# The split of the expert weights, moved: eight pieces of W1 early, W2 beside the groups, twelve pieces behind the last group

## The reference

```python
W = jnp.zeros((d, d)).at[rows, cols].set(w_est)
x = x + layernorm(x) @ W
z = layernorm(x);  xn = layernorm(z) * gamma + beta
w = softmax(top_2(xn @ Wr + br))                # 2 of 8 experts a row
for e in range(8):
    h = gelu(xn @ W1[e] + b1[e])                # 256 -> 512
    y = y + (h @ W2[e] + b2[e]) * w_full[e]     # 512 -> 256
x = x + y
```

## Time and profile before

| what | us |
|---|---|
| median of 3 runs | 1062.63 (1062.45 to 1066.76) |
| the profiled execution | 1061.05 |
| its span, first to last instruction | 1059.3 |
| PE busy | 900.6 |
| DVE busy | 753.9 |
| ACT busy | 633.8 |
| POOL busy | 627.9 |

### The profile page before, as it was taken

How to read it: one execution, slowest core, us unless ns; L and a number is a source line. 1 busy time by engine, 2 the same in 40 slices (tenths; PEclk the granted TensorE clock), 3 DMA queues, 4 the chain that set the end, 5 groups by cost and what they waited for, 6 DMA issues and landing times. The chain is left out here.

```text
span 1059.3 us, 25594 instructions
## 1 busy us (share of the span) xinstructions
PE 900.6 (85%) x6756; PEld 840.9 (79%) x6757; DVE 753.9 (71%) x2315; ACT 633.8 (60%) x1325; POOL 627.9 (59%) x490
## 2 busy tenths in 40 slices
PE   2583889898886029999999999999999999999992
PEld 1123777787775029999999999999999999999992
DVE  6985798999973507777777777777777777777761
ACT  2254666667662006776776776676676676677661
POOL 3664077777777743475565665665666564656653
PEclk9696899889986559999999999999999999999996
DMA  5055376766734533455544644544544554544542
GB/s 159 22 158 168 87 220 200 232 200 221 240 140 159 178 127 76 81 90 86 93 80 79 101 80 81 95 83 81 97 82 81 89 90 80 96 83 81 91 70 30
DMA packets 96231, 121.47 MB, mean 115 GB/s; under 512 B 15256, under 2 KB 73792, under 8 KB 96060
## 3 DMA queue, kind: packets, MB, share of 16 engines
q0 software_dynamic: 39904, 53.56, 29.0%
q1 hardware_dynamic: 55976, 66.58, 21.7%
q10 hardware_dynamic: 308, 0.85, 0.3%
HBM read 51.94 MB, written 69.00 MB: 114 GB/s over the span
## 5 line engine op out<-in xcount | busy, mean ns | idle before, releaser
L578 POOL DMA_INDIRECT out_dram<-ysb,yid x210 | 379.9, 1809 | 285.8 <-ACT ysb L1349 136.0
L749 PE MATMUL psum<-xh,w1s 128*128 128x256 f32 x1680 | 310.9, 285 | 0.0
L749 PEld LDWEIGHTS psum<-xh,w1s 128*128 128x128 f32 x1680 | 257.1, 189 | 0.0
L562 POOL DMA_INDIRECT slots<-arena_z,pos x196 | 191.6, 978 | 89.9 <-issue 59.1
L762 PE MATMUL psum<-w2h,hl 128*128 x840 | 237.5, 283 | 0.0
L762 PE MATMUL psum<-w2l,hh 128*128 x840 | 237.3, 283 | 0.0
L762 PE MATMUL psum<-w2h,hh 128*128 x840 | 237.2, 282 | 0.0
L749 PE MATMUL psum<-xl,w1s 128*128 128x256 f32 x840 | 235.2, 280 | 0.0
L1164 DVE TENSOR_TENSOR hl<-hact,hh 128x512 fp32r<-128x512 f32 x210 | 145.8, 694 | 87.9 <-ACT hh L1211 87.6
L1211 ACT ACTIVATE xh<-psum 128x512 fp32r<-128x512 f32 x105 | 62.7, 597 | 222.2 <-PE psum L736 222.2
L1332 ACT ACTIVATE hact<-psum,b1T 128x256 f32<-128x256 f32 x420 | 174.6, 467 | 14.3 <-PE psum L749 2.8
(11 more groups left out here) (187 smaller groups left out, 1119.9 us busy)
## 6 DMA issues: line engine op xcount, KB each, us to landing
zin<-slots SPq DMA_DIRECT2D x105, 260.0 KB
arena_x<-in_x_dram SPq DMA_DIRECT2D x14, 512.0 KB, 5.7
out_dram<-arena_s SPq DMA_DIRECT2D x14, 512.0 KB, 3.4
arena_z<-in_L_ffn_W_dram SPq DMA_DIRECT2D x24, 256.0 KB, 2.9
arena_x<-in_x_dram SPq DMA_DIRECT2D x13, 384.0 KB, 4.6
out_dram<-arena_s SPq DMA_DIRECT2D x13, 384.0 KB
out_dram<-ysb,yid POOLq DMA_INDIRECT x210, 4.2
slots<-arena_z,pos POOLq DMA_INDIRECT x196
```

The lines of the kernel that those rows point to most:

```text
L562: pool.indirect_dma_start(slots[:, :], bass.IndirectOffsetOnAxis(ap=pos[b][0:n, k, s:s + 1], axis=0), zg[b][0:n, s, :], None).then_inc(sen ...
L578: pool.indirect_dma_start(out[:, :], bass.IndirectOffsetOnAxis(ap=yid[u % MB][:, n:n + 1], axis=0), ysb[u % YB][:, n, :], None, compute_op ...
L749: last = nc.tensor.matmul(bank[2 + 2 * b + q][:, m * PAIR:(m + 1) * PAIR], w1s[b][:, w, k, hb * P:(hb + 1) * P], xs[b][:, k * PAIR:(k + 1) ...
```

## The change

SP loads eight pieces of W1 into eight buffers of their own as soon as the edges have landed, ahead of the first x tiles. TensorE's product with beta becomes columns: four products of 128x128 weights with one column of beta for each piece, four pieces ahead of the round's row products and four behind them. ScalarE scales a piece in place after TensorE has read it. GpSimd makes these eight lows only after `table_ready`. Twelve pieces of W2 go through two buffers, one beside each group from group 2 on: SP loads, ScalarE copies at the end of its group, DVE subtracts at the end of its group. The remaining four pieces of W2 and eight of W1 run behind the last group through five buffers, with DVE making the lows: five ahead of the last routing, seven behind the tables. TensorE does the beta columns of five of these W1 pieces ahead of the count and of three behind the tables. The bias is added on DVE just before the expert stage; the way through DRAM goes away.

```diff
+EARLY = 8
+W2B = 2
+BESIDE = GROUPS - 2
+LATE = [(2, n) for n in range(BESIDE, PIECES)] + [(1, n) for n in range(EARLY, PIECES)]
+LB = 5
@@ SP
+            def load_w2(n):
+                b = n % W2B
+                if n == 0:
+                    sp.wait_ge(w1_low, EARLY)
+                wait_from(sp, w2_low, n + 1 - W2B)
+                sp.dma_start(stage2[b]..., piece2(n)).then_inc(stage2_in[b], 16)
+            def load_late(m):
+                b, (w, n) = m % LB, LATE[m]
+                if m < W2B:
+                    sp.wait_ge(w2_low, BESIDE - W2B + m + 1)
+                elif m < LB:
+                    sp.wait_ge(xT_mm, NP * GROUPS)
+                else:
+                    sp.wait_ge(late_low, m - LB + 1)
+                    if LATE[m - LB][0] == 1:
+                        sp.wait_ge(late_read, m - LB - (PIECES - BESIDE) + 1)
...
+            for h in range(2):
+                sp.wait_ge(raw_in[h], 32 * len(EPARTS))
+            for n in range(EARLY):
+                sp.dma_start(stage[n], piece1(n)).then_inc(stage_in[n], 16)
+            sp.wait_ge(block_turned, EBLK)
...
             for g in range(2, GROUPS - 3):
+                load_w2(g - 2)
                 turn_over(g, g % 2)
...
+            for m in range(LB):
+                load_late(m)
             sp.wait_ge(g_added, NP * GROUPS)
...
+            for m in range(LB, len(LATE)):
+                load_late(m)
...
+            sp.wait_ge(late_low, len(LATE))
+            sp.wait_ge(late_read, PIECES - EARLY)
@@ GpSimd
-            low2(HALF, E // 2)
+            pool.wait_ge(table_ready, 1)
+            for n in range(EARLY):
+                low1(n)
@@ TensorE
+            def bias_columns(out_, w_, n):
+                e, k = n // KD, n % KD
+                for hb in range(KH):
+                    at = E * KH * k + KH * e + hb
+                    last = nc.tensor.matmul(out_[:, at:at + 1], w_[:, hb * P:(hb + 1) * P], bet[:, k:k + 1], start=True, stop=True)
+                return last
...
+            bias(0, EARLY // 2)
             pe.wait_ge(n_max_ready, 1)
...
                 last.then_inc(rows_ready, 1)
+                if early:
+                    bias(EARLY // 2, EARLY)
...
             ranks(GROUPS - 1)
+            late_bias(0, 2 * LB - 1)
             pe.wait_ge(routed, GROUPS)
...
             pe.wait_ge(tables_ready, 1)
-            pe.wait_ge(w_low, 2 * PIECES)
+            late_bias(2 * LB - 1, len(LATE))
@@ DVE, end of group(g)
+                if g > 2:
+                    low2(g - 3)
+                if g == GROUPS - 1:
+                    low2(g - 2)
...
             for _ in place(GROUPS - 2, (GROUPS - 2) % RZ):
                 pass
+            for m in range(LB):
+                low_late(m)
             for _ in route(GROUPS - 1, (GROUPS - 1) % RZ, full=False):
                 pass
...
+            for m in range(LB, len(LATE)):
+                low_late(m)
@@ ScalarE
             group(0, 0, z_side=False, older=False)
-            high2(HALF, E // 2)
-            act.wait_ge(w_low, 2 * PIECES)
             group(1, 1, older=False)
+            act.wait_ge(w1_low, EARLY)
+            act.wait_ge(w1_read, EARLY)
             for g in range(2, GROUPS):
                 group(g, g % 2)
+                high2(g - 2)
             group(GROUPS, 0, x_side=False)
+            for m in range(LB):
+                high_late(m)
             exp_gap(GROUPS - 1)
+            for m in range(LB, len(LATE)):
+                high_late(m)
```

## The result

The changed kernel takes 1051.47 us (median of 4 runs, 1051.03 to 1052.80) against 1063.31 for the kernel before beside it: a ratio of 0.9886, with a 95% interval of 0.9865 to 0.9907. Its profiled execution took 1051.4 us with a span of 1049.7, where the one of before had 1059.3.

A forecast was written before the change was run, and what follows sets the result against it. GpSimd's issue of 196 scatters was taken to bound the group stage, with DVE setting the time ahead of the first scatter. Gains of 5.9 + 4.0 + 4.7 = 14.6 us led to 1046.5 us, range 1042 to 1055.

The forecast's parts named there:

- Rival 1: In the winner rounds TensorE runs at its low clock: 4.9 us of the gain missing, 1051 to 1053; chance 0.11.
- rival 2: The tail behind the groups becomes the bound once its late chain is 2.1 us longer: 1050 to 1055; chance 0.14.
- (a): Ahead of the winner rounds, DVE's 128x8 comparison, freed of GpSimd's subtractions, returns from 7.03 to 0.17 us: gain 6.86 us.
- (b): TensorE's one-column bias products, 0.214 us an instruction, 32 ahead of the round's row products: 1.0 us of delay.
- rival 3: One-column bias products cost more than forecast: gain about gone at 0.41 us each, about 1072 at 0.5; chance 0.06.
- (c): The eight winner rounds that build the edge table shrink from 27.46 to 23.5 us: gain 4.0 us, at TensorE's high clock.
- (d): In group 0's statistics GpSimd's lows no longer hold five DVE instructions: gain 4.7 us, passed on whole.
- (e): Beside the groups, added loads, copies and DVE subtractions cost the scatters zero; far end 16.6 us for 24 subtractions.
- Rival 4: DVE's two-operand subtractions hold the scatters: 16.6 us lost, about 1063, no change; chance 0.04.
- (f): Behind the last group, twelve pieces make the tables 8.4 to 9 us later; 2.1 us of cover remain, no cost.

The follow-up runs named there:

- the kernel of the three edits: The changed kernel with two bias pieces ahead of the row products and six behind, DVE's subtractions from PSUM, and casts waiting for all scatters: 1047.51 us.

## Why the prediction came out as it did

It gave 1046.5 us and a range of 1042 to 1055; 1051.47 lies in the range, on the side of faster, but outside the 1043 to 1050 to which it gave 0.62. That the range took it in is luck: its upper part was kept for rivals 1 and 2, and the 5 us went elsewhere. Measured on the profiled executions the load came 9.0 us earlier, not 14.6: 10.7 up to the flag (9.9 forecast) and 4.7 in group 0 make 15.4 at group 1's normalization, and from these 1.4 are lost up to the first scatter, 4.8 in the scatters' stretch and 0.1 behind it. (The medians differ by more, 11.8, as the profiled execution of before, 1061.05, lay 2.3 below its median.)

- **(a) right.** The comparison reads 0.17.
- **(b) right in the size of an instruction; the delay was mostly something else.** 32 instructions in 6.96 us are 0.2175 each (0.214 forecast), so rival 3 was out. The comparison starts 1.7 us later than before, not 1.0; other executions of the same code have 0.3 to 1.9. Only 0.4 of the 1.7 is the queue that the prediction counted, as the row products start at 27.48 instead of 27.08. The rest is how long they ran at TensorE's low clock. The third of their four pairs, in the timelines of before (granted 1.00 from 30.4 on) and of after:

```profile
30.49 1.02 PE L635 MATMUL psum<-arena_z,ones 128*128 128x512 f32 x2
```
```profile
31.04 1.91 PE L656 MATMUL psum<-arena_z,ones 128*128 128x512 f32 x2
```

  A pair took 2.07 in before at a granted 0.50 and 1.02 at 1.00. In after three of the four were slow, in before two, in the kernel with the late subtractions cut (0.3 us of delay) one and a half. The profile gives no lower clock for after in this stretch, so its level is read from these durations.
- **(c) gain 4.95, forecast 4.0.** Eight rounds in 22.5 us: 3.01 apart, as GpSimd had held rounds 5 and 6 of before a little after all. Rival 1 came true for the products of the first two rounds alone: these eight took 6.37 us, in every later round four took 1.98.
- **(d) right.** From the flag to group 1's normalization 19.18 us instead of 23.85, 4.67 less. From there to the first scatter it is 30.29 us, 28.86 before, within the spread of 28.2 to 30.9. First scatter 119.82, forecast 118 to 120.
- **(e) wrong: the term that failed.** The subtractions were priced at zero, by one row of the expert stage in which a scatter takes its usual time with a subtraction inside it. In that row the scatter had started 0.23 us before the subtraction. That is the harmless order. The other order stood in the same trace of before, in the timeline of the same stage:

```profile
450.91 0.69 DVE L1164 TENSOR_TENSOR hl<-hact,hh 128x512 fp32r<-128x512 f32 x1 [0.27 <-ACT hh L1211]
451.03 2.02 POOL L578 DMA_INDIRECT out_dram<-ysb,yid  x1 [3.55 <-issue]
```

  With the subtraction first the scatter takes 2.02 instead of 1.56. It is no single case. Leaving aside the scatters that meet a copy of W1, 30 of that stage start more than 0.05 us behind the start of such a subtraction: 27 are held, until 0.10 to 0.13 us before its end, and the other three came in its last 0.08 us. Of the 77 that start with it or up to 0.60 us ahead of it none is over 1.59. So the trace that the prediction read settled the term against it; one row of the harmless order and the shortest scatter of the line (1.56; the longest took 2.52) could not show it. In after the 24 subtractions cost 5.06 us: four of the twelve in the groups hold a scatter for 0.34 to 0.40 (1.44), the late ones once each for 0.34, 0.53 and 2.75. Worked out from these rows, a single subtraction of 0.69 holds a scatter that starts up to 0.57 us behind it, which of one scatter each 1.274 us are 45%, for half of that on average: 0.13 us each, 1.5 for twelve. Rival 4 had the mechanism at 16.6, three times too dear, with a chance of 0.04.
- **(f) right.** ScalarE ended group 13 at 327.28, 13.4 us earlier than before; by the chain of (f), shifted by this, the count comes at 344.1 and the last filler is issued at 368.7. Measured: 343.72 and 367.41. The load came 10.8 us behind that issue, not 5.1, because the scatters ended 9.1 us earlier and not 14.6. So rival 2 didn't come here; it came, with 2.4 us, in the kernel of the three edits, whose scatters end 17.5 us earlier than those of before.

The Trainium skill ("GPSIMD Engine Reference", Specifications) had the side of this that the prediction's row seemed to deny: DVE instructions with two SBUF inputs contend with GpSimd. The kernel with PSUM operands (191.71 for 196.45) agrees. That it is the order of issue which decides who waits, as the Trainium skill ("SBUF — State Buffer", Who interferes with whom) puts it, agrees with the spaced subtractions (0.97 and 2.39), and not with the copies of W1 below, which hold scatters that started first.

## What to carry to other kernels

A row shows that two instructions don't disturb each other only for the order in which they started: look for the same pair the other way round, and at the whole spread of the line, before pricing an overlap at zero. A gain far ahead of a steady stream (196 scatters here) arrives only if nothing in the change touches the stream itself; compare the stream's own length, first start to last end, and not the span. Where two engines meet at SBUF, an operand that passes through PSUM, two products a piece and 48 in all, removed the whole loss of the stretch.

## What the runs showed of the hardware that was not expected

Five scalar_tensor_tensor in a row let no scatter in between them: it was held for 2.75 us, until 0.12 before the end of the fifth. Two tensor_tensor in a row did (328.06: 1.31 us beside a pair of 1.29, the hold ending with the first). And the casts, DVE's copies of W1 with one SBUF operand, hold a scatter that had started first, as the kernel with PSUM operands shows in its timeline:

```profile
367.14 1.79 POOL L575 DMA_INDIRECT slots<-arena_z,pos  x1 [0.30 <-issue]
367.59 2.36 DVE L1235 CAST w1s<-w 128x2048 fp32r x2 [1.33 <-issue]
369.24 1.51 POOL L575 DMA_INDIRECT slots<-arena_z,pos  x1 [0.30 <-issue]
```

The scatter started 0.45 us ahead of the first cast and took 0.82 too long. So the rule of order holds here for subtractions with two operands and not for these copies. The expert stage of before bears this out. Its 63 scatters that start behind the start of a cast are all held, by 0.15 to 0.95 us; and of the 25 that start with one or ahead of one, the 14 with the cast 0.42 to 1.17 us behind them are held too, by 0.20 to 0.91, as here in the timeline, and the nine with the cast 1.25 us or more behind them are not:

```profile
576.80 2.40 POOL L578 DMA_INDIRECT out_dram<-ysb,yid  x1 [3.36 <-issue]
577.90 1.22 DVE L1158 CAST w1s<-w 128x2048 fp32r x1
```

So a subtraction with two SBUF operands stops a scatter at its start alone, and a copy later in it as well. That the one stops what the scatter reads first and the other what it does later would fit; no run shows what the scatter does at either point.
